# Fetching a group's first tile in the middle of the group ahead of it

## What is computed

```python
x = x + 0.5 * ffn(layernorm(x), ...)
x = x + attn(layernorm(x), w_attn, w_o)
x = x + 0.5 * ffn(layernorm(x), ...)

def attn(x, w_attn, w_o):          # windows of W = 128 tokens, each sees itself and the one before
    q, k, v = split(x @ w_attn.T); q = q / W
    sim = where(keep, einsum(bq, bk2), 0)
    return einsum(square(relu(sim)), bv2) @ w_o.T

def ffn(x, ...):
    x_norm = layer_norm(x, in_gamma, in_beta)
    thought = x_norm[:, -1, :] @ agg_w + agg_b          # of the last token alone
    for _ in range(4):
        t = gelu(layer_norm(thought) @ d1_w + d1_b)      # 1024 -> 4096
        thought = thought + (t @ d2_w + d2_b)            # 4096 -> 1024
    broadcast = thought @ bc_w + bc_b
    return layer_norm(x + sigmoid(x @ gate_w + gate_b) * broadcast, out_gamma, out_beta)
```

## Time and profile before

| | us |
|---|---|
| median of 3 runs | 2033.42 (2031.25 to 2034.07) |
| the profiled execution | 2035.73 |
| its span | 2034.5 |
| PE busy | 1958.1 |
| DVE busy | 1262.6 |
| ACT busy | 696.5 |
| DMA traffic | 555.80 MB |

### The profile page before, as it was taken

How to read it: one execution, slowest core, us unless ns; L and a number is a source line. 1 busy time by engine, 2 the same in 40 slices (tenths; PEclk the granted TensorE clock), 3 DMA queues, 4 the chain that set the end, 5 groups by cost and what they waited for, 6 DMA issues and landing times.

```text
span 2034.5 us, 31033 instructions
## 1 busy us (share of the span) xinstructions
PE 1958.1 (96%) x12136; PEld 1036.5 (51%) x12136; DVE 1262.6 (62%) x2286; ACT 696.5 (34%) x1025; POOL 169.5 (8%) x278
## 2 busy tenths in 40 slices
PE   7998999999999999999999999999999999999997
PEld 3333444344434447665665655566655664444443
DVE  2322687324343567678787757666566637888887
ACT  1578546213223332223333122221122213444442
POOL 0000011000000010010100000000000001111111
PEclk9999999999999999999999999999999999999999
DMA  9589997889999863369979899989989966555552
GB/s 366 204 329 370 336 337 261 318 306 368 370 362 377 311 229 107 104 222 288 335 261 335 308 311 309 352 295 309 362 269 307 349 234 184 156 155 156 151 150 73
DMA packets 275216, 555.80 MB, mean 273 GB/s; under 512 B 149040, under 2 KB 149248, under 8 KB 274688
## 3 DMA queue, kind: packets, MB, share of 16 engines
q1 hardware_dynamic: 275072, 553.83, 78.5%
HBM read 406.93 MB, written 113.26 MB: 256 GB/s over the span
## 4 chain that ended last, share of the span: by engine, by line
PE 57%; DMA 11%; DVE 9%; SPq 2%; issue 1%; ACT 1%; POOL 1%; DVEq 0%; ACTq 0%
PE product_banks L1101 45%; PE product_banks L1136 4%; DMA thought_units<-parts_scratch 3%; PE thought_acc L1300 3%; PE product_banks L1235 2%; PE thought_acc L1290 2%; DMA gate_arena<-arena 2%; DMA thought_units<-in_d_w 2%; DVE bn_parts L1537 2%; DMA arena<-gate_scratch 1%; DMA arena<-qk_scratch 1%; SPq L1022 1%; DVE thought_units L1936 1%; SPq L884 1%; DVE arena L1713 1%
## 5 line engine op out<-in xcount | busy, mean ns | idle before, releaser
L1101 PE MATMUL product_banks<-gate_arena,arena 128*128 128x512 f16 x1536 | 353.6, 385 | 0.0
L1101 PE MATMUL product_banks<-wide_a,thought_units 128*128 128x512 f16 x1536 | 331.7, 379 | 0.0
L1101 PE MATMUL product_banks<-gate_arena,wide_a 128*128 128x256 f16 x2688 | 306.4, 275 | 9.4 <-DMA gate_arena<-arena 9.4
L1101 PE MATMUL product_banks<-wide_b,gate_arena 128*128 128x512 f16 x1344 | 299.2, 379 | 0.0
L1101 PEld LDWEIGHTS product_banks<-gate_arena,wide_a 128*128 128x128 f16 x2688 | 262.8, 99 | 57.0 <-issue 23.5
L1101 PEld LDWEIGHTS product_banks<-gate_arena,arena 128*128 128x128 f16 x1536 | 149.0, 99 | 197.8 <-issue 40.9
L1101 PEld LDWEIGHTS product_banks<-wide_a,thought_units 128*128 128x128 f16 x1536 | 150.3, 98 | 181.2
L1101 PEld LDWEIGHTS product_banks<-wide_b,gate_arena 128*128 128x128 f16 x1344 | 129.4, 98 | 157.6 <-issue 11.3
L1537 DVE BATCH_NORM_STATS2 bn_parts<-arena 128x6 f32<-128x512 f32 x256 | 164.3, 684 | 4.5
L2000 POOL TENSOR_TENSOR token_stats<-stats,minus_half 128x1 f32<-128x1 f32 x96 | 67.5, 703 | 988.0 <-DVE stats L1545 814.6
L1562 DVE SCALAR_TENSOR_TENSOR arena<-product_banks,inverse_gate,arena 128x512 f32<-128x512 f32 x64 | 47.8, 749 | 139.4 <-PE product_banks L1101 129.5
(11 more groups left out here) (221 smaller groups left out, 2365.5 us busy)
## 6 DMA issues: line engine op xcount, KB each, us to landing
thought_units<-parts_scratch SPq DMA_DIRECT2D x275, 512.0 KB, 7.8
thought_units<-in_d_w SPq DMA_DIRECT2D x174, 512.0 KB, 7.0
arena<-in_x SPq DMA_DIRECT2D x64, 512.0 KB, 9.3
parts_scratch<-thought_units SPq DMA_DIRECT2D x64, 512.0 KB, 6.1
x_scratch<-arena SPq DMA_DIRECT2D x64, 512.0 KB, 8.9
thought_row<-in_d_w SPq DMA_DIRECT2D x50, 512.0 KB, 7.2
arena<-x_scratch SPq DMA_DIRECT2D x40, 512.0 KB, 7.4
gate_scratch<-arena SPq DMA_DIRECT2D x32, 512.0 KB, 8.2
```

The lines of the kernel that those rows point to most:

```text
L1101: mm = pe.matmul(bank, left(i, k), right(j, k), start=(n == 0), stop=(n == 3 * KD - 1))
```

## The change

The fetch is now asked for by tile, not by group. The first tile of group n+2 is fetched in the list of prep steps of group n+1, right after the second tile's `x1_store`. The second tile is fetched where both were fetched so far, at the head of a group. At the start, tiles 0 and 1 are fetched together as before.

```diff
@@ plan_prep
         out += [("prep_norm", u), ("prep_h", u), ("rest",), ("prep_beta", u), ("prep_y", u), ("rest",), ("prep_x1", u),
-                ("prep_stats", u), ("rest",), ("x1_store", u), ("prep_h1", u), ("rest",), ("prep_low", u),
-                ("group_turn", u)]
+                ("prep_stats", u), ("rest",), ("x1_store", u)]
+        if i and u + 1 < TILES:
+
+            out.append(("prep_fetch", u + 1))
+        out += [("prep_h1", u), ("rest",), ("prep_low", u), ("group_turn", u)]
@@ plan_stage_2
-        out += [("prep_fetch", n + 1)]
+        out += [("prep_fetch", (n + 1) * GROUP + 1)]
@@ whole_plan
-    splits += [("prep_fetch", 0), ("rest",), ("rest",), ("prep_norm", 0), ("prep_beta", 0)]
+    splits += [("prep_fetch", 0), ("prep_fetch", 1), ("rest",), ("rest",), ("prep_norm", 0), ("prep_beta", 0)]
@@ sync_program, "prep_fetch"
-                n, = a
-                for u in (n * GROUP, n * GROUP + 1):
-                    s = u % PREP_RING
-                    if n == 0:
...
+                u, = a
+                s = u % PREP_RING
+                if u < PREP_RING:
+                    sp.wait_ge(fold_out[s], 16 * (2 * KD // FOLD_RING))
+                    sp.wait_ge(split_done, split_total("vo"))
+                else:
+                    sp.wait_ge(x1_out[s], 16 * (u // PREP_RING))
+                    sp.wait_ge(h1_ready, u - PREP_RING + 1)
+                    sp.wait_ge(y_made, u - PREP_RING + 1)
+                sp.dma_start(px_slots[s], x_flat[row_of(TILE_OF[u]), :]).then_inc(px_in[s], 16)
+                sp.wait_ge(gate_out[u % GATE_RING], 16 * (u // GATE_RING + 1))
+                if u >= PREP_RING:
+                    sp.wait_ge(group_in[s], 16 * (u // GROUP))
+                sp.dma_start(pg_slots[s], gate1_dram[row_of(TILE_OF[u]), :]).then_inc(pg_in[s], 16)
```

## The result

| | before | after |
|---|---|---|
| median, us | 2032.34 (4 runs, 2025.26 to 2034.07) | 2061.6 (4 runs, 2057.93 to 2062.59) |
| ratio, 95% interval | | 1.0145 (1.0125 to 1.0165) |
| profiled span | 2034.5 | 2059.6 |

What follows compares the result with a forecast made beforehand. TensorE (PE) was taken to bound the kernel. PE's stalls +30.8 us and clock +5.1, less 5.0 back, make net +30.9 on the median of 2033.42: 2064.3 us, range 2034 to 2082.

Steps and rivals of the forecast that it cites:

- Where PE stands: Sign in stage 2: PE's waits for gate_arena<-arena rise from 9.4 us to some 40, longest at q(7), q(11), q(12).
- (a): First tile's two fetches now stand ahead of each second turn in SP's queue: 2 x 1.3 = 2.6 us later.
- (b): prep_h1, prep_low and group_turn of second tiles come one step later; turn ready some 1.0 us later, counted at nothing.
- (c): In groups 7, 11 and 12 group_turn falls behind 4 more thought transfers, 6 with the fetch: 7.8 us.
- The margins: Time from the turn's landing to PE's start, absorbing delay: 1.4 us in group 5, 1.5 in 11, 0.1 in 12.
- The clock: Groups 8, 11 and 12 get stalls of the size followed by the low clock: 3 x 1.7 = 5.1 us.
- (d): x and gate of first tiles lie ready: 2.5 us back, and 2.5 from PE's shorter waits for thought units.
- Faster: Rival: turn late through the prep chain, not the queue; earlier x and gate pull it forward, 2018.9 us; chance 0.13.
- Milder: Rival: only the two fetches have their price, the four thought transfers none: +13.6, 2047 us; chance 0.20.
- Nothing: Rival: first tile's fetch waits on SP for its slot, x as late as now, within 4 us of 2033.4; chance 0.07.
- Worse: Rival: price 1.6 per transfer, twice the low clock after long stalls, nothing back: 2082 us and beyond; chance 0.05.

Runs made afterwards that it cites:

- e1: Kernel before, with the first tile's two fetches issued inside the second tile's x1_store step, list of prep steps unchanged; ratio 1.0047, 2038.83 us.
- e2: Kernel before, with an empty step where the change puts the fetch, both fetches staying at the head of the group; ratio 1.0088, 2049.82 us.
- e7: Kernel before, with the first tile's fetches issued by ACT on its own queue at the place of the second tile's x1_store; ratio 1.0036.
- e8: Kernel before, with the second tile's turn of groups 2 to 15 issued by ACT on its own queue, two waits added; ratio 1.0453, 2123.15 us.

## Why the prediction was right

The forecast was 2064.3 us, and 2061.6 was measured. The mechanism is the one that it named, and e1 and e2 bear out its two parts one by one; that the number is so near is in part luck, as the end of this section shows. Point by point:

- **Where PE stands.** It said waits for the turn of some 40 us, longest at q(7), q(11) and q(12) with 6 to 11 us each. It is 35.2, with 6.92, 5.39 and 7.46; group 11 is just under the 6 us, and group 13 with 5.37 is as long.
- **(a), two transfers, 2.6 us per turn.** e1 has 1.9. The price was read rightly: the two loads of the earlier trace rows landed at 1459.59 and 1460.86, 1.27 us apart. But it was oversized for this use, since two transfers put ahead of a turn made it only 0.93 us later each. That some of them drain before the turn is issued would explain it; this is argued and not shown. Groups 5, 6, 11 and 13 agree with 2.6 (+2.5 to +3.1 in e1), groups 8 and 12 have +2.0 and +1.6, and groups 4 and 7 do not agree (-0.5 and +0.8).
- **(b), counted at nothing.** Right but for group 13: in the other groups where nothing else moved, e2 has no more wait at q than before, while group 13 waits 1.6 us longer. Groups 1, 2, 9, 10 and 14 hide it.
- **(c), four transfers, 5.2 us.** Right for groups 11 and 12, of which e2 has +7.3 and +4.3, 5.8 on the mean. Both hold more than time in the queue: the turns were issued 3.6 and 2.6 us later, and from issue to landing the four loads made 3.7 and 1.7 us. So the sum fits and the statement that SP's wait costs nothing is not borne out. Wrong for group 7: +3.9 in e2, and +3.9 in the changed kernel with six transfers, and its stall grew by 3.5 us and not by 7.8. Two of the four were stores, and SP had to wait for their data. Its timeline in the changed kernel:

```profile
1130.31 0.32 SPq L1030 DMA_DIRECT2D x_scratch<-arena  x1
...
1139.98 0.32 SPq L981 DMA_DIRECT2D parts_scratch<-thought_units  x1
...
1141.59 0.43 SPq L887 DMA_DIRECT2D thought_units<-parts_scratch  x1
1142.12 7.19 SPq L1024 DMA_TRANSPOSE gate_arena<-arena  x1
```

  SP stood from 1134.8 us, the end of the loads before, to 1139.98. The turn landed 9.30 us after its issue in place of 10.80, with six transfers more ahead of it: while SP waited, the queue drained. I had added the price of all six transfers, as if the queue stayed full while SP stood. A wait of SP and a queue ahead overlap; they are not to be summed.
- **The margins.** Group 5 lost 2.5 us where 1.2 stood, and group 6 1.1 where 0 stood: the turn lands 4.0 and 3.1 us later behind its store there as well, and in group 6 the earlier prep gave nothing back. Group 8 lost 0.7 and not 2.6, since its `x1_store`-to-landing grew by 1.4 only. The eight places together: +25.8 for 30.8.
- **The clock.** Mis-sized the other way: +7.3 for 5.1. I took one stretch of 3.4 us per stall, as in the earlier trace rows. After four of the stalls of 5.3 us and more the low clock lasted 6.83 us.
- **(d), 5.0 us back.** 2.5 for thought units was 4.2. The other 2.5, for x and gate that lie ready, has no place in the account: with it left out the terms already give +28.9 for +28.5. That ACT's and DVE's 240 us were worth nothing is the main point of the case, and here I had still allowed them something.

The errors cancel: -5.0 in the waits, +2.2 in the clock, +0.8 for what came back, together -2.0 against a forecast of +30.9. Inside the waits they cancel too, since group 7 and group 8 lost 6.2 us less than forecast and groups 5, 6 and 13 2.8 us more. That is luck; the named mechanism is not.

**The rivals.** Faster needed the second turn within some 5 us of its issue; it took 9.3 to 17.2 in the loaded groups. Milder, the four transfers without price, falls with e2. Nothing falls with ACT's 14.5 us: x did come early. "Worse" named a second low-clock stretch per long stall; that part came true, at 2.2 us and not 5.

## What to carry to other kernels

Before a transfer is moved ahead, look up what will stand behind it in its queue and how much margin that has; x and gate had 178 and 83 us of waits that no one needed, the turn behind them had 0.1 to 1.5 us. A step put into a list that deals work out at a fixed pace moves all behind it, and what these pass may cost more than the step itself (0.88% for an empty one here, 0.47% for the fetch). Where a queue is full, measure from the last fixed point ahead of the victim to its landing, with and without the edit: adding a price per transfer to a wait of the issuing engine counts the same time twice.

## What the runs showed of the hardware that I had not expected

- A DMA transpose put on a queue of its own, beside a full one, lands later than in the full one: 16.2 us on the median and up to 25.8, against 10.5 and 14.4 for the same fourteen turns of the kernel before. A plain load on that queue lands sooner: in e7, from 824 to 1700 us, 13 x loads on ACT's queue took 5.7 us on the median, and 13 on SP's queue 8.9.
- On SP's queue the wait for the transfers ahead is for the most part in the issue of the transpose: in every run its landing is 1.4 to 3.7 us behind the end of the issue. In e8 on ACT's queue it is up to 22.5 us behind it.
- The engine that issues a transpose stands while it does so: 1.3 us where the DMA engines are nearly idle (at 824.6 us of the kernel before; their share is 0.06 from 823 to 826), up to 15.1 us on SP in the changed kernel, and up to 12.0 on ACT in e8, whose queue had no other transfers in it. On SP that holds up DMAs only; on ACT it held up copies that PE needed.
- Stalls of 2.4 to 3.4 us were followed by 3.4 us of the low clock, and four of the five over 5 us by 6.83 us; the fifth, of 5.37 us, by 3.41 (the kernels before and after). The experiments do not keep to this: 4.00 and 4.84 us in e2 and 4.21 in e1 were followed by 6.83 us, 4.92 in e2 and 4.94 in e1 by 3.41, and 2.69 in e7 by none. With 25.8 us more of waits for the turn the clock took 7.3 us more.
- Stage 1 is not equally long in each execution. The turn of tile 0 was issued at 733.9 us before, 732.8 after, 728.0 in e1 and 735.8 in e2, and up to there the order of the transfers and of ACT's and DVE's instructions is the same in all four. Up to the turn of tile 4 the low clock lasted 34.1, 30.7, 20.5 and 37.5 us in them, so it has the larger part of the difference. A difference of a few us between two profiled spans is better measured inside the stage that was changed.
